# Putting the last layer's columns in order by indirect stores of GpSimd instead of by products of TensorE

## The reference, cut to what matters

```python
def _L1_ffn_ref(x, up, down, perm):
    h, d = up.shape[0], up.shape[1]          # 16 heads of 64 columns
    unperm = jnp.argsort(perm)
    t = x.reshape(b * l, Dm)[:, perm]        # columns picked by perm
    t = t.reshape(b * l, h, d)
    t = jnp.einsum('bhd,hdm->bhm', t, up)    # 64 -> 256 in each head
    t = jax.nn.gelu(t, approximate=False)
    t = jnp.einsum('bhm,hmd->bhd', t, down)  # 256 -> 64
    t = t.reshape(b * l, h * d)[:, unperm]   # columns put back in order
    return t.reshape(b, l, Dm)
...
x = x + _L1_ffn_ref(_layernorm(x, axis=-1), L1_ffn_up, L1_ffn_down, L1_ffn_perm)
```

## Time and profile before

| | |
|---|---|
| median of 3 runs | 383.94 us (383.87 to 384.13) |
| the profiled execution, its own time | 383.87 us |
| its span, from first to last instruction | 382.1 us |
| the difference (start and end around the span) | 1.77 us |
| granted TensorE clock | 0.999 of full speed |
| PE, DVE, ACT, POOL busy | 91%, 71%, 52%, 32% of the span |

### The profile page before, as it was taken

One profiled execution on the slowest core, in us unless ns is written; L12 is line 12 of the kernel. 1 busy time (PEld: TensorE's weight loads), 2 busy tenths in 40 slices (PEclk: granted clock), 3 DMA queues, 4 the chain that ended last, 5 costly groups with the idle time before them and its releaser, 6 DMA issues.

```text
span 382.1 us, 5181 instructions
## 1 busy us (share of the span) xinstructions
PE 346.7 (91%) x1996; PEld 223.9 (59%) x1996; DVE 271.5 (71%) x352; ACT 199.0 (52%) x397; POOL 121.3 (32%) x96
## 2 busy tenths in 40 slices
PE   0688999999899989999999979799999989899996
PEld 0335444654566656566754857588443467787785
DVE  2867067757887999998975589887820699976381
ACT  1980223179999688688702664554010379252160
POOL 2600000025999888798920020201000020210000
PEclk9999999999999999999999999999999999999999
DMA  6999999563003011166137789399999997000001
GB/s 252 421 424 407 350 422 383 208 218 112 2 1 112 0 60 51 50 211 240 50 107 237 324 333 425 120 334 332 341 420 423 409 421 307 2 3 0 0 3 55
DMA packets 12967, 81.86 MB, mean 214 GB/s; under 512 B 2109, under 2 KB 2365, under 8 KB 3661
## 3 DMA queue, kind: packets, MB, share of 16 engines
q1 hardware_dynamic: 11614, 78.23, 52.9%
q10 hardware_dynamic: 1296, 3.22, 2.5%
q0 software_dynamic: 32, 0.07, 0.0%
HBM read 80.86 MB, written 0.52 MB: 213 GB/s over the span
## 4 chain that ended last, share of the span: by engine, by line
PE 63%; DVE 15%; POOL 10%; DMA 6%; ACT 3%; issue 2%; SPq 0%; DVEq 0%; ACTq 0%; POOLq 0%
PE psum L1021 13%; PE psum L973 10%; PE psum L1141 7%; PE psum L1242 6%; DMA ring<-in_ctx 6%; PE psum L1097 5%; POOL arena L620 5%; PE psum L980 5%; PE psum L935 4%; PE psum L1165 3%; DVE rounded L1646 2%; DVE arena L1603 2%; POOL arena L623 2%; PE psum L1396 2%; PE psum L1361 2%; POOL plain L620 2%
## 5 line engine op out<-in xcount | busy, mean ns | idle before, releaser
L770 ACT ACTIVATE arena<-arena 128x126 f32<-128x126 f32 x256 | 76.5, 388 | 9.8 <-DVE arena L1603 8.8
L1021 PE MATMUL psum<-ring,hT 128*128 128x512 f32 x128 | 60.6, 602 | 0.8 <-ACT hT L686 0.8
L1603 DVE TENSOR_TENSOR_SCAN arena<-arena,psum 128x1024 f32<-128x1024 f32 x24 | 54.2, 2273 | 3.3 <-PE psum L1097 3.0
L560 POOL TENSOR_TENSOR small<-small 128x1 f32<-128x1 f32 x6 | 9.3, 1553 | 133.0 <-DVE small L1446 127.4
L620 POOL TENSOR_TENSOR arena<-arena 128x1024 f32<-128x1024 f32 x20 | 47.2, 2361 | 5.4 <-DVE arena L1603 5.4
L1646 DVE TENSOR_TENSOR rounded<-ring,rounded 128x2048 fp32r<-128x2048 f32 x16 | 36.5, 2286 | 10.2 <-ACT rounded L797 10.1
L1141 PEld LDWEIGHTS psum<-arena,ident 128*128 128x128 f32 x292 | 35.6, 192 | 13.8 <-issue 10.0
L797 ACT ACTIVATE rounded<-ring 128x2048 fp32r<-128x2048 f32 x16 | 30.6, 1912 | 24.8 <-PE psum L980 15.3
L1141 PE MATMUL psum<-arena,ident 128*128 128x128 f32 x292 | 37.3, 278 | 1.5 <-POOL arena L623 1.5
L1021 PEld LDWEIGHTS psum<-ring,hT 128*128 128x128 f32 x128 | 22.2, 190 | 27.1 <-issue 26.0
L1097 PE MATMUL psum<-plain 64*128 64x512 f32 x128 | 36.1, 641 | 1.7 <-DVE arena L1603 1.4
(11 more groups left out here) (213 smaller groups left out, 581.2 us busy)
## 6 DMA issues: line engine op xcount, KB each, us to landing
ring<-in_w_in SPq DMA_DIRECT2D x16, 1024.0 KB, 14.1
ring<-in_ctx SPq DMA_DIRECT2D x13, 1024.0 KB, 11.9
ring<-in_w_out SPq DMA_DIRECT2D x8, 1024.0 KB, 4.8
ring<-in_ctx_t SPq DMA_DIRECT2D x7, 1024.0 KB, 6.4
ring<-in_w_base SPq DMA_DIRECT2D x4, 1024.0 KB, 4.8
ring<-in_x_wk SPq DMA_DIRECT2D x4, 1024.0 KB, 7.9
ring<-in_a_wo SPq DMA_DIRECT2D x4, 1024.0 KB, 10.9
ring<-in_x_wq SPq DMA_DIRECT2D x3, 1024.0 KB, 8.9
```

The lines of the kernel that those rows point to most:

```text
L770: last = act.activation(to, of, ACT.Exp, scale=a_par[:, k, state_no:state_no + 1])
L1021: last = pe.matmul(psum[:, proj_bank(j), :], hT[:, k, :], slot(w_in + u)[:, k % UK, :], start=(k == 0), stop=(k == KT - 1))
L1603: dve.tensor_tensor_scan(state[s % STATES], dA[:, s % 3, :], psum[:, p:p + 2, :].rearrange("p a b -> p (a b)"), 0.0, ALU.mult, ALU.add).th ...
```

## The change

The MLP's output is no longer turned back. The output tensor in HBM becomes `(1024, 128)`, one row of 512 bytes for each column of `x`, and the host turns it at the end. The picked columns of `x` itself are now wanted in the same transposed form: the picked product plus `mean` gives them (`same`), TensorE turns them into banks 2 and 3, VectorE copies them (`sameT`) and adds them to the MLP's output (`y_outT`). Eight indirect stores of GpSimd, one for each block of 128 rows, write row `perm[r]` of the output from row `r`.

```diff
@@ memory and semaphores
-        perm_col = carve(small, 296, KT)
-        iota = carve(arena, 10336, D)
+        same = carve(arena, 9312, D)
+        sameT = carve(arena, 10336, KT, P)
-        y_out = carve(arena, 6144, D)
+        y_outT = carve(arena, 6144, KT, P)
@@ SyncE
-            for nh in range(2):
-                sp.wait_ge(y_ready, nh + 1)
-                cols = slice(nh * UN, nh * UN + UN)
-                sp.dma_start(out[:, cols], y_out[:, cols]).then_inc(out_done, 16)
-            sp.wait_ge(out_done, 32)
+            sp.wait_ge(out_done, 16 * KT)
@@ GpSimd
-            pool.iota(iota, pattern=[[1, D]], base=0, channel_multiplier=0,
-                      allow_small_or_imprecise_dtypes=True).then_inc(iota_ready, 1)
-            pool.tensor_copy(perm_col, perm_coli).then_inc(perm_f, 1)
             rstd_of(5)
+            for k in range(KT):
+                if k % 4 == 0:
+                    pool.wait_ge(y_ready, k // 4 + 1)
+                pool.indirect_dma_start(out=out[:, :], out_offset=bass.IndirectOffsetOnAxis(ap=perm_coli[:, k:k + 1], axis=0),
+                                        in_=y_outT[:, k, :], in_offset=None).then_inc(out_done, 16)
@@ ScalarE
             act.activation(picked[:, 0:UN], psum[:, 4, :], ACT.Copy, scale=rstd[:, 5:6]).then_inc(picked_lo, 1)
+            act.activation(same[:, 0:UN], psum[:, 4, :], ACT.Identity, bias=mean).then_inc(same_lo, 1)
-            act.wait_ge(down_psum, 1)
-            act.activation(split[:, 0, 0:4, :], psum[:, 0, :], ACT.Copy).then_inc(o_high, 1)
@@ TensorE
-            for half in range(2):
-                pe.wait_ge(picked_hi if half else picked_lo, 1)
-                transpose4(6 + half, picked, UN * half, gT_turned)
+            pe.wait_ge(picked_lo, 1)
+            transpose4(6, picked, 0, gT_turned)
+            pe.wait_ge(same_lo, 1)
+            transpose4(2, same, 0, same_turned)
+            pe.wait_ge(picked_hi, 1)
+            transpose4(7, picked, UN, gT_turned)
             for a in range(MH // 2):
                 pe.wait_ge(g_hi if a >= 4 else g_lo, 1)
+                if a == 2:
+                    pe.wait_ge(same_hi, 1)
+                    transpose4(3, same, UN, same_turned)
+                if a >= 4:
+                    pe.wait_ge(same_copied, a // 2 - 1)
-            for nh in range(2):
-                for part, signal in enumerate((o_high, o_low)):
-                    for k in range(KT):
-                        ... (waits)
-                        last = pe.matmul(psum[:, 2 + nh, :], split[:, part, k, :], onehot[:, k, UN * nh:UN * nh + UN],
-                                         start=(part == 0 and k == 0), stop=(part == 1 and k == KT - 1))
-                last.then_inc(placed, 1)
@@ VectorE
             dve.tensor_scalar(picked[:, halves(1)], psum[:, 5, :], rstd[:, 5:6], None, ALU.mult).then_inc(picked_hi, 1)
+            dve.tensor_scalar(same[:, halves(1)], psum[:, 5, :], mean, None, ALU.add).then_inc(same_hi, 1)
-            (eight calls that write onehot from iota and perm_col; the splits; the additions of x)
+            for half in range(2):
+                dve.wait_ge(same_turned, half + 1)
+                dve.tensor_copy(sameT[:, 4 * half:4 * half + 4, :], psum[:, 2 + half, :]).then_inc(same_copied, 1)
+            for half in range(2):
+                v = slice(4 * half, 4 * half + 4)
+                dve.wait_ge(down_psum, half + 1)
+                dve.tensor_tensor(y_outT[:, v, :], psum[:, half, :].rearrange("p (k t) -> p k t", k=4), sameT[:, v, :],
+                                  ALU.add).then_inc(y_ready, 1)
@@ host
-    out = nc.dram_tensor("out", (P, D), F32, kind="ExternalOutput").ap()
+    out = nc.dram_tensor("out", (D, P), F32, kind="ExternalOutput").ap()
-    return result.results[0]["out"].reshape(B, L, D)
+    return np.ascontiguousarray(result.results[0]["out"].T).reshape(B, L, D)
```

More of the change, by code:

```diff
@@ L393, in perceiver @@
         perm_f = sem("perm_f")
-        iota_ready = sem("iota_ready")
         pick_ready = sem("pick_ready")
-        place_ready = sem("place_ready")
         g_psum = sem("g_psum")
@@ L405, in perceiver @@
         down_psum = sem("down_psum")
-        o_high = sem("o_high")
-        o_low = sem("o_low")
-        placed = sem("placed")
+        same_lo = sem("same_lo")
+        same_hi = sem("same_hi")
+        same_turned = sem("same_turned")
+        same_copied = sem("same_copied")
         y_ready = sem("y_ready")
@@ L1733, in _ @@
                                           accum_out=qbias))
-            dve.wait_ge(perm_f, 2)
+            dve.wait_ge(perm_f, 1)
             dve.wait_ge(tables_in, 16)
```

## The result

| | before | after |
|---|---|---|
| median of the runs | 384.02 us (383.87 to 384.13) | 385.42 us (385.20 to 385.57) |
| ratio of the times | | 1.0036 (95% interval 1.0024 to 1.0048) |
| the profiled execution's own time | 383.87 us | 385.57 us |
| its span | 382.1 us | 383.8 us |
| granted TensorE clock, mean | 0.999 | 0.989 |

The kernel became 0.36% slower, 1.4 us. The clock needs one remark: it falls to 0.5 of full speed, the 1.2 GHz level, only from about 375.6 us on, when TensorE's last product had been over for three microseconds. So it cost nothing.

What follows compares the result with a forecast made beforehand. TensorE's own pace bounds the chain at the end. First GpSimd store at 371.05, plus 9.6 for eight stores and 2.25 of tail, gives span 382.9 against 382.1; 383.87 + 0.8 = 384.7 us, range 381.5 to 389.

Steps and rivals of the forecast that it cites:

- the two halves of a store's price: GpSimd's indirect store: 0.78 us as for the plain tables' load, plus 0.34 for reading row numbers and 0.08 pause.
- TensorE up to half of `down`: Last layer: eight more transposes make TensorE run 0.6 us later, bounds 0.5 to 0.9.
- addition's end to first store: First half's addition ends at 370.99 and GpSimd's first store starts at 371.05.
- eight stores: GpSimd's queue at the end: eight indirect stores, 1.2 us each, take 9.6 us (6.2 to 12.5).
- last issue to the end: Tail behind the last store: 1.2 lag, 0.2 data, 0.86 to span's end, about 2.25 us (1.5 to 5.25).
- The first four transposes: Lower half of `same`, mostly hidden in TensorE's wait for VectorE's upper half: +0.1 us.
- The four inside `up`: The other four added transposes, with nothing to hide them: +0.5 us.
- Rival (a): Cheap stores, faster: 0.78 to 1.00 us each on GpSimd; 382.3 us with 0.9; chance 0.25.
- (c): Dear stores, slower: GpSimd needs over 1.4 us each; 387.6 us with 1.56, 394.3 with 2.4; chance 0.14.
- (d): Row by row: each row number read by its own access; near 462 us or some 725; chance 0.03.
- rival (b): Late landing, slower: the 4.2 us lag belongs to GpSimd's queue and shows behind the last store; 387.7 us; chance 0.14.
- What would show it: Signs: first store at 371.0 to 371.4, pitch 1.2 us; wrong if a much longer first store or gap before the fifth.

Runs made afterwards that it cites:

- the half-rows run: The changed kernel with each of the eight indirect stores writing only partitions 0 to 63, half of the output unwritten: 384.74 us.
- the block version: The late-turn version with `down` products, additions and signals by blocks of 128 columns, each in its own PSUM bank, one block awaited per store: 384.88 us.
- the interleaved one: The block version with `down` for blocks 0 and 1 put ahead of `up` 6 and 7: 384.10 us.
- the one still earlier: The interleaved one with `down` 0 moved behind `up` 3 and `down` 1 behind `up` 5: 385.44 us.
- the last: The interleaved one with the second turn, then `down` 0 and 1, behind the fourth `up` step; both turned halves copied before the first addition: 382.54 us.
- the late-turn version: The changed kernel with the four transposes of the upper half of `same` moved from inside `up` to behind `down`: 384.64 us.

## Why the prediction held, term by term

Direction, place and mechanism were right: GpSimd's eight issues eat what TensorE gave up. That the size came out so near is in part luck: the two halves of a store's price, and two parts of the landing, were wrong in opposite directions. The forecast was 384.7 us with a range of 381.5 to 389.0, the median is 385.42; growth was forecast at 0.8 us and measured at 1.4. By the profiled executions, the terms against the trace:

| term | predicted | trace | differs |
|---|---|---|---|
| ahead of the last layer | 0 | +0.35 | +0.35 |
| TensorE up to half of `down` | +0.6 | +0.82 | +0.22 |
| addition's end to first store | 0.06 | 0.30 | +0.24 |
| eight stores | 9.6 | 9.98 | +0.38 |
| last issue to the end | 2.25 | 1.97 | -0.28 |
| span | 382.9 | 383.8 | +0.9 |

- **Ahead of the last layer.** `transpose_h(5)` starts at 353.88 against 353.53. 0.2 us of it is there in the first microseconds: ScalarE gets the first load of `ctx` at 9.39 against 9.19 (9.21 to 9.44 in the experiments). Over the eleven experiments `transpose_h(5)` starts at 353.61 to 353.83, all later than before. The edit touches nothing there; whether this is scatter of the first load or belongs to the changed program is open.
- **TensorE.** The first four transposes are hidden more fully than foreseen: in the chain `up` begins at 364.36 against 363.97, 0.39 later, of which 0.35 is the shift above; 0.04 is left where 0.1 was forecast. The four inside `up` cost more: `up` and turn take 4.56 us together (364.29 to 368.85) against 3.78, so 0.78 for 0.5. The transposes are 0.59 of it; the rest is what `up` loses when it is cut in two (its weight loads wait 0.17 us for "issue" where it takes up again). `down` is no longer than before: its first half is used 2.01 us after its first product, against 2.02. 0.04 + 0.78 = 0.82 stands inside the bounds of 0.5 to 0.9.
- **Hand-over.** The 0.06 rested on no row of a DMA; the nearest row, a GpSimd arithmetic instruction behind VectorE, has 0.09. The trace has 0.30 here, and 0.28 to 0.31 in every run in which GpSimd's first DMA waited for an addition. The step that failed is taking a DMA's start to be as quick as an arithmetic instruction's.
- **The stores.** 1.27 for 1.2 is close, but its parts were wrong in opposite directions: 0.55 for a plain store, not 0.78; 0.72 for being indirect, not 0.42. Of the pitch, 0.30 isn't in the listed duration at all. So 1.2 was near by luck: the plain part was 0.23 too dear and the indirect part 0.30 too cheap. Rival (a) rested on the suspicion that the tables' 0.78 holds a cost of the program's start. The 0.55 fits it but does not prove it, since the tables' load also goes the other way and has longer rows; and the indirect part more than made up for it. Rivals (c) and (d) fall with 0.96 listed and the half-rows run.
- **Landing.** The 4.2 us of rival (b) did not recur: 0.54 us to the first data, near the SyncE store's 0.45, where the prediction took 1.2. From the last data to the end are 1.23 instead of 0.86. The one error made up for about half of the other. The Trainium skill's page "DMA: Bandwidth & Descriptors" (section "Latency and other measured facts") gives about 1 us to the first byte; the trace has 0.54 from the end of the issue and 1.50 from its start, so the figure lies between and depends on where one starts to count. Its direction against the tables' row was right.
- **What would show it.** First store 371.0 to 371.4: missed, 371.85, by the shift and the hand-over. Pitch 1.2: 1.27. A longer first store: 0.18 us. Gap before the fifth: none.

## What to carry to other kernels

A product whose only work is to permute can be worth less than the instructions that take its place: count them at their pitch, on the queue that issues them, not by bytes (64 KB each moved in 0.2 us here, the issue took 1.27). When such a queue becomes the end of the chain, move its start forward and have everything that its later members need done first; that turned 0.36% slower into 0.36% faster. And price a DMA from a row late in the program, if there is one: GpSimd's first DMA, a load, cost 0.78 us to issue and its data began over 4 us after that; a plain store of nearly the same size at the end cost 0.55, with its first data about half a microsecond behind the issue.

## What the runs showed of the hardware

- An indirect store of GpSimd: 0.96 us listed for 128 rows of 512 bytes, 0.89 for 64, and 0.30 ahead of each; a plain one of the same bytes 0.54 to 0.55 and no pause between two. The very first store is longer: 1.14 indirect, 0.66 plain. Landing 2.2 us (median) from the start of the issue, against 1.8.
- A DMA of GpSimd starts 0.28 to 0.31 us after the VectorE instruction that it waited for, one of SyncE 0.03.
- While indirect stores were being issued, much of the work that waited for TensorE began 0.9 to 3.0 us after the trace shows the products ended (for the turned half 2.98 in the block version, 1.90 in the interleaved one, 0.94 in the one still earlier; for ScalarE 1.17 in the last). The semaphores themselves were raised late, by up to 3.49 us; with plain stores of GpSimd all eight of `down_psum` came 0.02 us after the products. A few signals that fell inside or behind the second indirect store were on time. In after and in the late-turn version nothing was late: there TensorE's last signals fell inside the first store or in the pause behind it. VectorE's own signals to GpSimd were never late. The cause is open.
